# Conditioning products moved behind the first transfers, VectorE readouts one scan later, and one readout per group moved from GpSimd to VectorE, in a Mamba layer followed by linear attention

## The reference

```
ada  = silu(c) @ ada_w.T + ada_b                  # c: 64 x 1024; ada: 64 x 1536
shift, scale, gate = split(ada, 3)
xn   = layernorm(x) * (1 + scale) + shift
x_in, z = split(xn @ in_proj_w.T, 2)              # 1024 channels each
u    = silu(causal_conv4(x_in) + conv_b)
dt_r, B, C = split(u @ x_proj_w.T, [64, 80])      # B and C: 16 states
dt   = softplus(dt_r @ dt_proj_w.T + dt_proj_b)
h_t  = h_(t-1) * exp(dt_t * A) + (dt_t * u_t) * B_t      # 1024 channels x 16 states
y_t  = sum over states(h_t * C_t) + u_t * D
x1   = x + gate * ((y * silu(z)) @ out_proj_w.T)
# second layer: x1 + film_out(silu(layernorm(attention(layernorm(x1))) * (1 + scale2) + shift2))
# scale2, shift2 = split(silu(c) @ film_emb_W + film_emb_b, 2)      # FiLM
```

## Time and profile before

| | |
|---|---|
| Median of 3 runs | 4882.42 us (4878.9 to 4889.22) |
| Profiled execution, its own time | 4885.56 us |
| Its span | 4883.8 us |
| Busy over the span: PE, DVE, ACT, POOL | 90%, 85%, 64%, 82% |
| Body of `mamba`, first to last GpSimd instruction | 110.82 to 3686.40 us |
| Granted TensorE clock over the span | 0.98 of full speed |

### The profile page before, as it was taken

One profiled execution on the slowest core, in us unless ns is written; L12 is line 12 of the kernel. 1 busy time (PEld: TensorE's weight loads), 2 busy tenths in 40 slices (PEclk: granted clock), 3 DMA queues, 4 the chain that ended last, 5 costly groups with the idle time before them and its releaser, 6 DMA issues. The chain is left out here.

```text
span 4883.8 us, 74903 instructions
## 1 busy us (share of the span) xinstructions
PE 4403.5 (90%) x21856; PEld 3136.2 (64%) x21856; DVE 4136.2 (85%) x5011; ACT 3124.1 (64%) x7557; POOL 4009.9 (82%) x1861
## 2 busy tenths in 40 slices
PE   6898988888988989888888999898877999999998
PEld 4666666666666666666666666666655666665655
DVE  2999999999999999999999999999995666565664
ACT  2777777777777777777777777777763333333332
POOL 1999999999999999999999999999994434333342
PEclk8999999999999999999999999999988999999999
DMA  5111111111111111111111111111122222232221
GB/s 196 40 44 47 44 47 44 45 49 50 61 58 45 46 45 44 47 44 45 52 54 57 54 45 46 45 44 46 40 72 95 89 89 99 86 102 86 99 84 46
DMA packets 121580, 301.58 MB, mean 62 GB/s; under 512 B 15393, under 2 KB 20769, under 8 KB 120674
## 3 DMA queue, kind: packets, MB, share of 16 engines
q1 hardware_dynamic: 121186, 296.91, 18.0%
HBM read 245.35 MB, written 51.51 MB: 61 GB/s over the span
## 5 line engine op out<-in xcount | busy, mean ns | idle before, releaser
L671 POOL TENSOR_TENSOR dbu<-du,bc 128x1024 f32<-128x1024 f32 x1024 | 2418.6, 2406 | 108.3 <-DMA bc<-b_scratch 108.3
L432 ACT ACTIVATE dA<-dt,c_A 128x256 f32<-128x256 f32 x4096 | 1752.1, 467 | 448.4 <-DVE hC L575 399.6
L638 DVE TENSOR_TENSOR_SCAN hS<-dA,dbu 128x512 f32<-128x512 f32 x1024 | 1210.8, 1209 | 116.3 <-ACT dA L432 58.7
L682 POOL TENSOR_TENSOR hS<-hS,bc 128x1024 f32<-128x1024 f32 x512 | 1231.5, 2405 | 13.4 <-DVE hS L638 12.9
L638 DVE TENSOR_TENSOR_SCAN dA<-dA,dbu 128x512 f32<-128x512 f32 x1024 | 1207.2, 1212 | 20.6 <-ACT dA L432 13.4
L305 PEld LDWEIGHTS Y<-c_ident,hC 128*128 128x128 f32 x4096 | 477.5, 143 | 293.0 <-DVE hC L575 196.4
L305 PE MATMUL Y<-c_ident,hC 128*128 128x128 f32 x4096 | 551.4, 279 | 123.4 <-DVE hC L575 119.5
L575 DVE TENSOR_TENSOR hC<-dA,bc 128x1024 f32<-128x1024 f32 x512 | 626.7, 1224 | 27.0 <-DVE dA L638 5.4
L346 PE MATMUL side<-sh_weights,sh_tile 128*128 128x512 f32 x1024 | 508.1, 620 | 100.5 <-DVE u L601 58.4
L305 PE MATMUL Y<-c_ident,hS 128*128 128x128 f32 x4096 | 539.7, 275 | 12.8 <-POOL hS L682 12.7
L305 PEld LDWEIGHTS Y<-c_ident,hS 128*128 128x128 f32 x4096 | 479.5, 143 | 97.5 <-issue 62.6
(11 more groups left out here) (123 smaller groups left out, 5476.8 us busy)
## 6 DMA issues: line engine op xcount, KB each, us to landing
bc<-b_scratch SPq DMA_DIRECT2D x256, 512.0 KB, 4.0
sh_tile<-in_x SPq DMA_DIRECT2D x64, 512.0 KB, 6.0
o_scratch<-oS SPq DMA_DIRECT2D x64, 256.0 KB, 2.0
sh_tile<-o_scratch SPq DMA_DIRECT2D x32, 512.0 KB, 4.7
sh_tile<-gate_scratch SPq DMA_DIRECT2D x32, 512.0 KB, 5.7
x_scratch<-p_x_in SPq DMA_DIRECT2D x32, 512.0 KB, 3.2
p_xr<-x_scratch SPq DMA_DIRECT2D x32, 512.0 KB, 6.7
out<-p_xr SPq DMA_DIRECT2D x32, 512.0 KB, 3.0
```

The source lines that it names most:

```text
L432: last = act.activation(dA[:, q % A_RING, e, :], dt[j % 2][:, e, :], ACT.Exp, scale=C["A"][:, 2 * j + e, n:n + 1])
L638: dve.tensor_tensor_scan(out.rearrange("p e t -> p (e t)"), dA[:, q % A_RING, :, :].rearrange("p e t -> p (e t)"), dbu[(q // 2) % B_RING][ ...
L671: gps.tensor_tensor(dbu[p % B_RING][:, :, :, :], du[j % 2][:, :, :].unsqueeze(1).broadcast_to([P, 2, 2, GT]), bc[:, 0, n:n + 2, :].unsquee ...
L682: gps.tensor_tensor(h, h, bc[:, 1, n:n + 2, :].unsqueeze(2).broadcast_to([P, 2, 2, GT]), ALU.mult).then_inc(hcP_done, 1)
```

## The change

Three things are changed at once.

1. **Conditioning.** `setup` keeps only the shift and scale part of `ada` (16 products in place of 40, and 8 turns in place of 16). The FiLM matrix, the gate part of `ada`, the gate's bias and the output projection's weights are loaded last, the first three of them into buffers that the scans use later (`bc`, `hC`, `hS2`, `oS0`), and `setup` does not wait for them. TensorE makes the FiLM and gate products in groups -2 and -1; VectorE copies, turns them into `gm1`, `bm1` and makes the gate in groups -1 and 0.
2. **Order in the scans.** VectorE's readout of a D pair stands after the first scan of the next pair, no longer after its own second scan; the multiplication dt*u stands one unit after dt (`DU_AFTER`). ScalarE writes the four ACTIVATEs of a pair of units in a row, and the side work of two units (`beside`) after them; before, side work stood between the two ACTIVATEs of a unit too. u*D is made by ScalarE (`skip_values`, 8 more ACTIVATEs of 128x256 in a group), and TensorE only transposes it (4 transposes in place of 4 products for each quarter). The tables of places are new.
3. **`KINDS`.** In the last quarter of each group three pairs are of kind G and five of kind D, in place of four and four.

```diff
-KINDS = ["GGDGDGDD"] * 4
+KINDS = ["GGDGDGDD", "GGDGDGDD", "GGDGDGDD", "GDGDDGDD"]
...
-D_ACC = {4: [8, 11, 15, 17], 5: [6, 10, 11, 15, 17]}
-G_ACC = {4: [7, 10, 14, 17], 3: [7, 12, 17]}
+D_ACC = {4: [9, 12, 16, 18], 5: [9, 10, 12, 16, 18]}
+G_ACC = {4: [8, 10, 14, 17], 3: [8, 12, 17]}
...
-YZ_AT = [18, 34, 50, 66]
...
-DMM_AT = [6, 22, 38, 54]
+YZ_AT = [19, 35, 51, 67]
...
+DMM_AT = [8, 24, 40, 56]
+UD_AT = [1, 17, 33, 49]
...
             for b in range(GB):
                 for k in range(2):
-                    last = pe.matmul(Y[:, b, k * P:(k + 1) * P], u[par][:, 2 * j + k, b * P:(b + 1) * P],
-                                     W["skip"][:, 2 * j + k, :], start=(b == 0 and k == 0), stop=False, skip_group_check=True)
+                    last = pe.matmul(Y[:, b, k * P:(k + 1) * P], uD[:, k, b * P:(b + 1) * P], C["ident"][:, :],
+                                     start=(b == 0 and k == 0), stop=False, is_transpose=True, skip_group_check=True)
...
+                if at == -2 and q == 0:
+                    film_products(0, 8)
+                if at == -2 and q == 50:
+                    film_products(8, 11)
+                if at == -1 and q == 40:
+                    film_products(11, 16)
+                if at == -1 and q == 51:
+                    turn_film()
+                    gate_product()
+                if at == 0 and q == 0:
+                    pe.wait_ge(out_in, 16)
...
-                    if KINDS[j][p] == "D" and half == 1:
-                        readout(g, j, D_PAIRS[j].index(p))
                 for j in range(4):
+                    for m, p in enumerate(D_PAIRS[j]):
+                        t = 16 * j + 2 * p + 2
+                        if q == t % UNITS and inside(at, -(t // UNITS)):
+                            readout(g - t // UNITS, j, m)
...
+            for q in range(0, UNITS, 2):
+                if inside(at, 0):
+                    for i in range(2):
+                        bank_freed(act, g, q + i)
+                        if at == 0 and q + i == 0:
+                            act.wait_ge(film_taken, 2)
+                        if at == 0 and q + i == 3:
+                            act.wait_ge(gate_v, 1)
+                        if q % NST == 0 and i == 0:
+                            wait(act, dtc_done, g * 4 + (q // NST + 1))
+                        decay(g, q + i, 0)
+                        decay(g, q + i, 1)
+                beside(q)
+                beside(q + 1)
...
-        for k in range(KD):
-            sp.dma_start(W["in"][:, k, :], io["inT"].rearrange("(k p) n -> p k n", p=P)[:, k, :]).then_inc(weights_in, 16)
-        sp.dma_start(W["out"][:, :, :], io["outT"].rearrange("(k p) n -> p k n", p=P)).then_inc(weights_in, 16)
-        sp.wait_ge(weights_in, 16 * (7 + KD))
-        sp.wait_ge(gate_v, 1)
-        sp.dma_start(io["gate"], gate[:, :]).then_inc(gate_out, 16)
-        sp.wait_ge(gate_out, 16)
+
+        sp.dma_start(M["bc"][:, :, :, :].rearrange("p a n t -> p (a n t)").rearrange("p (k n) -> p k n", k=KC), film_v).then_inc(late_in, 16)
+        for k in range(KC):
+            sp.dma_start(gate_chunk(M, k), ada_v[:, k, 2 * D:3 * D]).then_inc(late_in, 16)
+        sp.dma_start(M["oS0"][0:NB, :], io["b_gate"].partition_broadcast(NB)).then_inc(gbias_in, 16)
+        sp.dma_start(W["out"][:, :, :], io["outT"].rearrange("(k p) n -> p k n", p=P)).then_inc(out_in, 16)
+        sp.wait_ge(weights_in, 16 * (6 + KD))
```

More of the change, by code:

```diff
@@ L434, in decay, with simple @@
                 last.then_inc(dA_ready, 1)
-        def simple(kind, j, src, own, par):
+        def simple(kind, j, src, own, par, part):
             wait(act, filled[kind], nth(kind, j, own))
@@ L491, in copy_dt, with skip_values @@
                            src[:, :].rearrange("p (e t) -> p e t", t=P)[:, :, 1:P], ACT.Copy).then_inc(dtc_done, 1)
+        def skip_values(g, j, par):
+            wait(act, u_done, g * 4 + (j + 1))
+            wait(act, dmm_done, g * 4 + j)
+            for k in range(2):
+                last = act.activation(uD[:, k, :], u[par][:, 2 * j + k, :], ACT.Copy, scale=C["dcol"][:, 2 * j + k:2 * j + k + 1])
+            last.then_inc(uD_done, 1)
         def take_y(g, j, par):
@@ L516, in stages, with beside @@
                         staged(kind, j, stage, bank[bk], tmp[(sig_base[of] + s) % 2], go + d, earlier(2, s, of, go, sigs_at))
[L518 to L527 removed]
+            def beside(q):
+                stages(q, 2, S2)
+                stages(q, 1, S1)
                 stages(q, 0, 0)
@@ L531, in body @@
                         copy_dt(j, bank[bk], go + d)
-                    if kind in ("XN", "XI", "XP", "O") and q == end + A_AFTER[kind] - off:
-                        simple(kind, j, bank[bk], go + d, (of + d) % 2)
+                    for part in range(2 if kind == "XN" else 1):
+                        if kind in ("XN", "XI", "XP", "O") and q == end + A_AFTER[kind] + 2 * part - off:
+                            simple(kind, j, bank[bk], go + d, (of + d) % 2, part)
                 for j in range(4):
+                    if q == UD_AT[j] and inside(at, 0):
+                        skip_values(g, j, at % 2)
                     t = YF_AT[j]
@@ L655, in body @@
                 for (kind, j, d, end, bk, s, off), of, go in side:
+                    if kind == "DT" and q == end + DU_AFTER - off:
+                        step_times_u(j, bank[bk], go + d, (of + d) % 2)
                     if kind in D_AFTER and q == end + D_AFTER[kind] - off:
```

253 lines of the change are left out of this document (147 added, 106 removed).

## The result

The changed kernel takes 4891.02 us in the median of 20 runs (4882.61 to 4897.0). The kernel before, on the same chip, takes 4883.52 us in 20 runs. The ratio is 1.0014, with a 95% interval from 1.0008 to 1.0019. That is slightly slower, but within the 0.2% that the prediction counts as no change (it gave that outcome a chance of 0.05), and 71 us above the forecast of 4820. It lies outside the range (4793 to 4866). The profiled execution of the changed kernel is its fastest run, 4882.61 us with a span of 4880.8 us.

The account below looks back on a forecast made before the run. GpSimd was taken as the bound, VectorE next, both near 109 us a group afterwards. 4885.6 less 57.6 (body, 109.9 us a group) and 5.2 (start) gives 4822.8, as a median 4820 us; range 4793 to 4866.

Parts of the forecast that it names:

- GpSimd's floor: Body: one readout of 48 GpSimd instructions goes, leaving 47 x 2.318 = 108.9 us a group, 2.4 us less.
- VectorE's terms: Body: 111.7 us a group plus 1.15 for the moved readout, less 1.6, 0.4, 1.0 and 0.5, giving 109.3.
- The fourth rival: VectorE: a dependent readout costs nothing extra, so 111.9 us a group and 4883 us, no change; chance 0.04.
- The ScalarE term: Body: decays late because D-pair buffers free one scan later; 0.6 us a group added, bounds 0 and 2.3.
- The slower rival: ScalarE late at each D pair: VectorE waits 0.25 us 17 times a group, about 4936 us; chance 0.10.
- The first rival: VectorE bounds with some ScalarE lateness: 1.0 to 2.2 us a group more, 4833 to 4871 us; chance 0.18.
- A single late decay costs little: Body: GpSimd's `dbu` ring of four lets it run on a few us; only repeated late decays cost all.
- That stall stays and is in the 109.3: Hardware loop's turn: VectorE stands 3.08 us, an estimated 40 us at 13 turns, already counted in VectorE's group time.
- The start: Before the body: x issued while late loads run, 6.5 us earlier, less 1.3 given back; 5.2 us less.
- the 1.3 us "given back": Start: five film products ahead of XP take 2.15 us where TensorE now waits only 0.85 us.
- The sign that I had named: VectorE's waits for ScalarE: about 90 us expected; past 150 us the prediction is wrong, the slower rival from there on.
- the third rival: Readout and GpSimd instruction exclude each other: moved readout waits 1.16 us, 111.1 us a group, 4858 us; chance 0.03.

Follow-up runs that it names:

- e11: Changed kernel with ScalarE's two pairs of XN copies together and 14 groups per hardware-loop turn in place of two: 4806.06 us, ratio 0.9839 to the kernel before.
- e8: Changed kernel with VectorE's readout back right behind the second scan of its own pair: 4895.46 us, ratio 1.0013 to the kernel before.
- e9: Changed kernel with XN copies together, second quarter's y turn at 36, and readout right behind the second scan: 4840.73 us, ratio 0.9903 to the kernel before.
- e6: Changed kernel with XN copies together and TensorE's turn of the second quarter's y at 36 in place of 38: 4839.76 us, ratio 0.9904 to the kernel before.
- e3: Changed kernel with ScalarE's two pairs of XN copies done together again: 4832.76 us, ratio 0.9893 to the kernel before.
- e4: Changed kernel with TensorE's turn of the second quarter's y at 36 in place of 38: 4858.07 us, ratio 0.9951 to the kernel before.
- e1: Changed kernel with the old KINDS, four G and four D pairs in the last quarter too: 4880.93 us, ratio 1.0002 to the kernel before.
- e7: Changed kernel with XN copies together, second quarter's y turn at 36, and the old KINDS (four G pairs): 4874.4 us, ratio 0.9971 to the kernel before.
- e12: Kernel before with 14 groups per hardware-loop turn in place of two: 4880.51 us, ratio 0.9989 to the kernel before.
- e10: Changed kernel with 14 groups per hardware-loop turn in place of two: 4846.81 us, ratio 0.9921 to the kernel before.

## Why the prediction was wrong

- **GpSimd's floor**, 47 x 2.318 = 108.9 us a group: right. e11 comes to 3501.9 / 32 = 109.4 us.
- **VectorE's terms.** The bubble ahead of the readout went as costed in the earlier trace rows, the `hS` wait for TensorE for the greater part (14.6 to 5.2 us), and VectorE's busy time fell from 106.3 to 105.4 us a group. But the step that made them a gain failed. e8 and e9 have no later readout and the same times as the changed kernel and e6. The fourth rival, that the later readout costs and brings nothing, has the right result by another cause: the bubble of 0.10 us is real (54.0 us over 544 readouts in e8), only no one waits for it.
- **The ScalarE term, 0.6 us: this is the step that failed.** The body took 3578.5 / 32 = 111.8 us a group, 2.5 us more than the 109.3 to which the term was added. I spread the lateness over the D pairs and called it small, since ScalarE is "mostly early". VectorE's waits for ScalarE rose by (172.3 - 72.1) / 32 = 3.1 us a group, above my bound of 2.3. What the term should have held is what reaches GpSimd: (91.7 - 13.4) / 32 = 2.4 us a group, which is the whole gain of the floor. A part of it is the loop turn, below; the rest comes from places where ScalarE's order puts a copy of a TensorE result ahead of decays. e3 shows 49.2 us of it, 1.5 us a group, at the XN copies, cut in two with the XI products already due; e4 shows 24.7 us at the second quarter's Y, which overlap with the first (e6). The slower rival, 0.25 us at each D pair, is refuted by e11, which has all the later readouts and a body of 3501.9 us. The first rival came nearer: lateness of ScalarE that eats the gain, though its 2.2 us a group at most were too few and its place was wrong.
- **"A single late decay costs little", because GpSimd's `dbu` ring lets it run on.** That held before, when GpSimd was the later engine by some us at each such place (e1, e7, e12: 14.1, 8.1 and 6.4 us idle). With 47 instructions GpSimd has next to no work behind which VectorE could be late, and it stands up to 3.1 us each time, 48.6 us in 30 groups.
- **"That stall stays and is in the 109.3".** It stayed, and what it costs was about right: the forecast body of 3517 us lies 31 us above GpSimd's floor (1504 x 2.318 = 3486.3), and GpSimd stands 31.6 us at the 13 turns. But it was right by another way than I wrote. I read it as a stall of VectorE in a sum of VectorE's, 3.08 us each time; in the kernel before, 12 turns less are worth 2.3 us each of VectorE's waiting and next to nothing of the time (e12), and in the changed kernel they are GpSimd's own idle time, 33.5 us (e10), because GpSimd no longer covers them.
- **The start**, 5.2 us: right to 0.7 us at the first `dbu`, wrong as a gain of the kernel. It was given back within 47 us, by the wait for XI in the first group; with the XN copies together (e11) it is kept. What VectorE's small instructions cost there was not separated. One reading in it was wrong: I took a row of the trace for a product, but each of these products stands there as two records (the 40 of before are 80 records, 48 of `ada` and 32 of `film`). So the eight film products took 9.25 us, at a mean clock of 0.76, and the five ahead of XP 4.51 us (from 91.77), in place of 3.4 and 2.15. That the 1.3 us "given back" came out (from x at VectorE to the first `dbu` 50.67 us, 49.42 before) is luck as far as these runs show.
- **The sum.** Forecast 3517 us for the body; the changed kernel has 3578.5. The 61.5 us between them are the 48.6 us at one readout of each group and the 10.0 us of the first group, nearly all. With the first place mended the forecast would have stood: e3 has a body of 3530.0 us and takes 4832.76. e11, without the loop turns too, lies 15 us below the forecast body.

The sign that I had named, VectorE's waits for ScalarE above 150 us, came (172.3), but with another meaning than I gave it. GpSimd's distance of 2.318 us held, so the third rival (GpSimd and VectorE excluding each other) is out.

## What to carry to other kernels

- When a change takes work from the engine that bounds, ask of each stall of the engines that feed it whether it was covered by that work. List the single long ones (here a loop turn of 3 us) apart from the average: with two engines near their floors each such stall counts in full, and a sum of averages doesn't show it.
- Price a change of order by the idle time of the bounding engine, not by the waits of the next one. The next one's waits for ScalarE can double with no cost (e1: 156.9 us against 72.1 before), or more than halve with no gain (e8: 73.4 against 172.3).
- In a schedule written as tables, compare the producer's unit with the consumer's for each pair that the change moves (XN's last copy at 52 for products at 50, a copy of Y at 37 for transposes at 38). An in-order engine that comes to a copy too early holds up all that stands behind it.
